# Negated row maxima turned by VectorE's 32x32 block transpose instead of TensorE, and written to the query stack by four transfers per half batch

## What is computed

```
attn = jnp.einsum('blhd,bmhd->bhlm', q, k) / scale
p = jax.nn.softmax(attn, axis=-1)
o = jnp.einsum('bhlm,bmhd->blhd', p, v).reshape(B, L, D)
```

## Time and profile before

| what | value |
|---|---|
| median of the runs | 1639.73 us |
| profiled execution's own time | 1638.78 us |
| span of its trace | 1637.0 us |
| TensorE matmul busy | 1542.3 us, 94% |
| VectorE busy | 1044.1 us, 64% |
| ScalarE busy | 779.4 us, 48% |
| GpSimd busy | 182.1 us, 11% |
| mean granted TensorE clock | 0.989 |

### The profile page before, as it was taken

The page is one execution under the profiler, slowest core; times in us unless marked ns, Lnnn a source line. Parts: engine busy times, 40 slices in busy tenths (PEclk is TensorE's granted clock), DMA queues, the critical chain, the costliest instruction groups (busy, mean ns, idle before and its releaser), DMA issues. The chain is left out here.

```text
span 1637.0 us, 30596 instructions
## 1 busy us (share of the span) xinstructions
PE 1542.3 (94%) x10971; PEld 1287.6 (79%) x11020; DVE 1044.1 (64%) x3343; ACT 779.4 (48%) x1684; POOL 182.1 (11%) x219
## 2 busy tenths in 40 slices
PE   2569999999999999999999999999999999999997
PEld 1458888888888888888888787887877778777785
DVE  7746555555555555555567767776676776767773
ACT  1335444444444444444445555555555555555554
POOL 7400000000000000000000000000001011110102
PEclk9789999999999999999999999999999999999999
DMA  7074222222222222221235445354453444444340
GB/s 264 7 91 66 44 40 46 46 40 44 47 46 47 47 47 41 37 52 31 40 67 66 69 60 70 51 70 66 60 73 57 76 73 66 85 64 83 69 71 21
DMA packets 99584, 100.09 MB, mean 61 GB/s; under 512 B 11478, under 2 KB 96088, under 8 KB 98794
## 3 DMA queue, kind: packets, MB, share of 16 engines
q1 hardware_dynamic: 99434, 98.14, 36.2%
HBM read 16.83 MB, written 4.19 MB: 13 GB/s over the span
## 5 line engine op out<-in xcount | busy, mean ns | idle before, releaser
L922 ACT ACTIVATE work<-bank 128x512 f32<-128x512 f32 x768 | 453.6, 600 | 244.1 <-PE bank L1116 201.2
L528 DVE TENSOR_REDUCE rowmax<-bank 128x2 f32<-128x512 f32 x512 | 342.9, 687 | 167.7 <-PE bank L1099 163.1
L1116 PE MATMUL bank<-qs,ks 98*128 98x256 f32 x1536 | 401.9, 344 | 0.9 <-DVE rowmax L528 0.6
L1099 PE MATMUL bank<-ks,qs 96*128 96x256 f32 x1536 | 349.8, 310 | 12.7 <-DMA ks<-qk_lo 10.3
L1116 PEld LDWEIGHTS bank<-qs,ks 98*128 98x128 f32 x1536 | 270.2, 192 | 33.2 <-issue 12.4
L1099 PEld LDWEIGHTS bank<-ks,qs 96*128 96x128 f32 x1536 | 243.7, 190 | 39.1 <-DMA ks<-qk_lo 14.7
L525 DVE CUSTOM_DVE_ANT_0 c1t<-bank,big_q 128x256 bf16<-128x256 f32 x512 | 190.4, 421 | 0.7 <-issue 0.7
L1128 PE MATMUL bank<-work,vp 128*32 128x256 f32 x3072 | 185.7, 382 | 0.0
L1128 PEld LDWEIGHTS bank<-work,vp 128*32 128x32 f32 x3072 | 89.9, 109 | 66.1 <-issue 6.0
L948 ACT ACTIVATE work<-bank 128x256 f32<-128x256 f32 x128 | 49.3, 385 | 192.3 <-PE bank L1175 192.3
L1175 PE MATMUL bank<-yt,w_gate 128*128 128x256 f32 x512 | 131.8, 379 | 2.1 <-ACT yt L942 2.1
(11 more groups left out here) (208 smaller groups left out, 1891.9 us busy)
## 6 DMA issues: line engine op xcount, KB each, us to landing
qs<-qk_hi SPq DMA_DIRECT2D x192, 128.0 KB, 3.9
ks<-qk_hi SPq DMA_DIRECT2D x192, 128.0 KB, 3.8
qs<-qk_lo SPq DMA_DIRECT2D x96, 128.0 KB, 4.3
ks<-qk_lo SPq DMA_DIRECT2D x96, 128.0 KB, 4.3
xres<-in_x_t SPq DMA_DIRECT2D x4, 1024.0 KB, 9.5
x_in<-in_x SPq DMA_DIRECT2D x16, 256.0 KB, 3.2
out<-xres SPq DMA_DIRECT2D x16, 256.0 KB, 2.1
qs<-nm SPq DMA_DIRECT2D x96, 16.0 KB
```

The source lines that it names most:

```text
L528: a = dve.tensor_reduce(rowmax[:, :, k:k + 1], bank[:, :].rearrange("p (t s) -> p t s", t=TC), AX, ALU.max)
L922: act.activation(probs[:, place[n, b, k], :, :], bank[:, :].rearrange("p (c s) -> p c s", c=TC), ACT.Exp, scale=HD ** -0.5)\
L1099: m = pe.matmul(bank[:, t * S:(t + 1) * S], qs[par][0:SCORE_ROWS, k, t * P:(t + 1) * P], ks[par][0:SCORE_ROWS, k, :], start=True, stop=True)
L1116: m = pe.matmul(bank[:, c * S:(c + 1) * S], ks[par][0:SHIFTED_ROWS, k, c * P:(c + 1) * P], qs[par][0:SHIFTED_ROWS, k, :], start=(n != 3), ...
```

## The change

`nm` and `negs` get the same shape of 128 partitions by 32 columns, with columns ordered (part, head, token tile). After L537 VectorE waits for the low part and for the earlier DMAs out of `nm`, and transposes each 32x32 block of `negs` in its own quadrant of 32 partitions into `nm` (new line L538, STREAM_TRANSPOSE). Row r of quadrant w then holds column r of `negs` for tokens 32w to 32w+31 of a tile. The two TensorE transposes, their bank use in the ring, and the copy L542 are gone. SP issues four DMAs for each half batch, one for each quadrant w; each writes pieces of 32 numbers (128 bytes) to rows 96 and 97 of `qs`, where the one DMA of before wrote runs of 256 numbers. The bytes are the same. `probs` waits for all four. `SLOT` and `LATER` get other numbers for several steps in all three layers.

```diff
+QUADS = P // HW
 SLOT:  (two of the lines, layer 2)
-        "smax": -14.7, "pv": (9.43, 16.76), "neg": (-6.67, 1.15), "max": (-6.24, 2.71), ...
+        "smax": -15.46, "pv": (9.43, 16.53), "neg": (-6.97, 0.53), "max": (-6.04, 2.71), ...
...
-        negs = [sb(f"negs{u}", [P, TC, 2 * HALF], F32R) for u in range(DC)]
-        nm = [sb(f"nm{u}", [2 * HALF, S], F32R) for u in range(DC)]
+        negs = [sb(f"negs{u}", [P, 2, HALF, TC], F32R) for u in range(DC)]
+        nm = [sb(f"nm{u}", [P, 2 * HALF * TC], F32R) for u in range(DC)]
...
-                self.shifted = [shared(f"shifted{u}", 16) for u in range(DC)]
+                self.shifted = [shared(f"shifted{u}", 16 * QUADS) for u in range(DC)]
...
-                if what == "max":
-                    return [(middle, f"max{k}", self.nm, k + 1)]
...
                     if what == "neg":
-                        top = rowmax[:, :, HALF * k:HALF * (k + 1)]
-                        hi, lo = negs[k][:, :, 0:HALF], negs[k][:, :, HALF:2 * HALF]
+                        top = rowmax[:, :, HALF * k:HALF * (k + 1)].rearrange("p t h -> p h t")
+                        hi, lo = negs[k][:, 0, :, :], negs[k][:, 1, :, :]
...
-                    if what == "max":
-
-                        bank = middle.wait_filled(dve, n, b, f"max{k}")
+                        dve.wait_ge(L.negs.sem, L.negs.at(b, 2 * k + 2))
                         dve.wait_ge(L.shifted[k].sem, L.shifted[k].at(b, 0))
-                        dve.tensor_copy(nm[k][:], bank[0:2 * HALF, 0:S]).then_inc(L.nm.sem, 1)
+                        dve.transpose(nm[k][:].bitcast(F32), negs[k][:].rearrange("p a h t -> p (a h t)").bitcast(F32)).then_inc(L.nm.sem, 1)
...
                     if what == "max":
                         sp.wait_ge(L.nm.sem, L.nm.at(b, k + 1))
-                        sp.dma_start(qs[par][SHIFT:SHIFT + 2, HALF * k:HALF * (k + 1), :].bitcast(F32), nm[k][:].bitcast(F32)).then_inc(L.shifted[k].sem, 16)
+                        shift = qs[par][SHIFT:SHIFT + 2, HALF * k:HALF * (k + 1), :].rearrange("p h (t w c) -> p h t w c", t=TC, w=QUADS)
+                        for w in range(QUADS):
+                            rows_w = slice(HW * w, HW * (w + 1))
+                            sp.dma_start(shift[:, :, :, w, :].bitcast(F32), nm[k][rows_w, :].bitcast(F32)).then_inc(L.shifted[k].sem, 16)
...
-                    if what == "max":
-
-                        pe.wait_ge(L.negs.sem, L.negs.at(b, 2 * k + 2))
-                        bank = middle.wait_free(pe, n, b, f"max{k}")
-                        for t in range(TC):
-                            m = pe.transpose(bank[0:2 * HALF, t * P:(t + 1) * P], negs[k][:, t, :].bitcast(F32), ident[:])
-                        m.then_inc(middle.sem, 1)
```

More of the change, by code:

```diff
@@ L38 @@
     1: {
-        "smax": -13.9, "pv": (8.35, 15.57), "neg": (-6.64, 1.59), "max": (-6.11, 3.88), "xT": -26.05, "q": -24.15,
-        "stack": (-25.3, -22.08, -15.9, -16.88), "k": -22.83, "v": -12.48, "tok": 18.52, "load": -46, "rank": -33,
-        "cond": -31.71, "squares": -30.67, "xn": -28.51, "oT": 20.77, "wo": 22.0, "yn": 23.31, "yT": 24.73,
+        "smax": -13.9, "pv": (8.35, 15.57), "neg": (-6.64, 2.63), "max": (-6.11, 3.88), "xT": -26.05, "q": -24.15,
+        "stack": (-25.3, -22.08, -15.9, -16.88), "k": -22.83, "v": -12.48, "tok": 18.52, "load": -46, "rank": -32.97,
+        "cond": -31.71, "squares": -30.67, "xn": -28.51, "oT": 20.77, "wo": 22.51, "yn": 23.31, "yT": 24.73,
         "ffn": (25.73, 1.15), "down": (26.94, 1.15)},
     2: {
[6 rows of a table removed]
-        "squares": 22.77, "resid": 24.18},
[6 rows of a table added]
+        "wo": 22.34, "squares": 23.07, "resid": 24.21},
 }
-LATER = {"vector": {"q": -0.2, "k": 0.5, "ffn": 0.3, "oT": 0.39, "field": -0.34, "pv": -0.22, "coh2": 0.07, "squares": 0.41}, "scalar": {"wo": 1.0, "pv": 0.2, "yn": -0.02, "oT": -0.25, "xn": -0.04, "ffn": -0.24, "xT": -0.5, "field": 0.3, "k": -0.14}, "gpsimd": {"max": -0.28, "oT": -0.2, "q": -0.42, "pv": -0.5}, "sync": {"wo": 0.39}}
+LATER = {"vector": {"q": -0.2, "k": 0.5, "ffn": 0.3, "oT": 0.39, "field": -0.34, "pv": -0.22, "coh2": 0.07, "squares": 0.41}, "scalar": {"wo": 1.0, "pv": 0.2, "yn": -0.02, "oT": -0.25, "xn": -0.04, "ffn": -0.24, "xT": -0.5, "field": 0.44, "k": -0.14, "squares": -0.13, "coh2": -0.04}, "gpsimd": {"max": -0.28, "oT": -0.2, "q": -0.42, "pv": -0.5}, "sync": {"wo": 0.39}}
 ONCE = {"ortho": -33.5, "top": -30.3, "shares": -26.5, "spread": -22.0}
@@ L1101, in step @@
                         m.then_inc(middle.sem, 1)
-                    if what == "max":
-                        pe.wait_ge(L.negs.sem, L.negs.at(b, 2 * k + 2))
-                        bank = middle.wait_free(pe, n, b, f"max{k}")
-                        for t in range(TC):
-                            m = pe.transpose(bank[0:2 * HALF, t * P:(t + 1) * P], negs[k][:, t, :].bitcast(F32), ident[:])
-                        m.then_inc(middle.sem, 1)
                     if what == "probs":
                         if k % HALF == 0:
-                            pe.wait_ge(L.shifted[k // HALF].sem, L.shifted[k // HALF].at(b, 16))
+                            pe.wait_ge(L.shifted[k // HALF].sem, L.shifted[k // HALF].at(b, 16 * QUADS))
                         bank = back.wait_free(pe, n, b, f"p{k}")
```

## The result

The changed kernel took 1627.26 us (median of 5 runs, 1624.28 to 1629.49) against 1639.73 us before (median of 5 runs): ratio 0.9928, 95% interval 0.9914 to 0.9943. It is 12.5 us faster. The forecast was 32 us faster, with a range of 1591 to 1624 us, so the direction was right and the size was wrong. The profiled execution took 1626.92 us, its span 1625.1 us.

What follows compares the result with a forecast made beforehand. TensorE was taken as the bound; 6.7, 11.8 and 16.2 us gained in layers 1 to 3 (34.7), less 3 for VectorE, gave about 32 us off 1639.7, so 1607.5 us, with an 8-in-10 range of 1591 to 1624.

Steps and rivals of the forecast that it cites:

- TensorE is the bound, and its freed slots are the gain: All layers: each pair of transposes leaving TensorE frees 0.21 us where nothing waits; 96 pairs, 20.2 us.
- The stall for the negation goes: Layers 2 and 3: TensorE's wait ahead of the transposes goes, 0.53 and 0.80 us in one half batch per batch.
- the first rival: TensorE's 15.8 us idle for the negation returns as waits for maxima or exponentials; gain only 20.2 us, 1619.5; chance 0.20.
- the give-back: Layer 3: VectorE is next to be late once TensorE no longer waits; 0.2 us a batch, 3 us in all.
- VectorE's part: VectorE swaps the 409 ns copy L542 for a block transpose of 200 ns, relieving it by some 20 us.
- SP's three more issues cost nothing: SP issues 1.95 us more per half batch; cost nothing, bounds -0.3 to +1.95 us a batch of layer 2.
- The one on SP's queue: Key stack pushed back the full 1.95 us, TensorE waiting that much more per layer 2 batch: +31 us, 1648 total; chance 0.07.
- Small pieces: Rival: 128-byte pieces double the nm transfers' landing to 5.8 us, delaying probs; 42 us in layer 2, 1659 total; chance 0.03.

Runs made afterwards that it cites:

- l3_stack_first: Changed kernel, but in layer 3 SP issues the key stack for heads 0 to 7 before the output store and four nm transfers: 1600.87 us, ratio 0.9775.

## Why the prediction was wrong

- *TensorE is the bound, and its freed slots are the gain.* Right in kind. The pair costs 0.21 us in layer 1, as forecast (5.2 us gained over 15 periods, 6.3 forecast). In layers 2 and 3 putting the pair back cost 0.12 and 0.11 us, not 0.21.
- *The stall for the negation goes.* Right: the row is gone. The idle time didn't come back as a wait for maxima on the matmul side, as the first rival had it. With the stack out of the way (l3_stack_first), layer 3 lost 16.4 us against before, where 15 of the 16 forecast periods come to 15.2 us. Layer 2 lost 15.8 us in the changed kernel, with 11.1 forecast for 15 periods. Once layer 3 doesn't wait, the span is 1637.0 - 1598.8 = 38.2 us shorter, where 34.7 less 3 given back to VectorE were forecast; the give-back isn't seen.
- *VectorE's part.* Right: 211 ns against 200 taken, and never over 214, though it stands next to negations of 1.22 us.
- *SP's three more issues cost nothing.* This is the step that failed, and by its second half. For layer 2 I counted from issue to need, found the margin nearly zero, and the new place of the negation covered it, as the rows after show (2.5 us of matmul wait against 2.0). For layers 1 and 3 I wrote that "no wait for the stack stands in the rows, and SP itself spends most of its time waiting, so I cost the issues at nothing there". Layer 1 bore it: its rows after have no wait for the stack. Layer 3 had 1.5 us of slack in the batch shown, took 1.2 us of later issue, 0.8 us of TensorE's own earliness and 0.5 us of later landing, and paid 18.3 us of waits in 13 batches. Its order put right (l3_stack_first) gives 24.8 us back: 18.4 of idle time, some 5 of lower clock by estimate, and a rest. So the term that stood at nothing measured about 25 us. The sum with it is 34.7 - 24.8 = 10 us, and 12.5 were measured.
- *The rivals.* The one on SP's queue was the right mechanism with 0.07 of the chance, priced in layer 2, where it cost little; of layer 3 it said only that lateness there would decide too. "SP waits most of the time" was no argument: its waits stand ahead of `nm` and of the store, and the stack is behind them.
- *Small pieces.* Their landing didn't double. In a batch of layer 2 of the kernel after (SyncE's issues and TensorE's weight load), the fourth issue ends at 999.79 and the `probs` that needs it starts at 1002.88 without a wait, so the fourth transfer lands within 3.1 us of the end of its issue, or 3.8 us of its start, where the one transfer of before landed within 2.9 us. A rise of up to 0.9 us isn't excluded:

```profile
997.14 2.65 SPq L681 DMA_DIRECT2D qs<-nm  x4
999.90 1.24 SPq L666 DMA_DIRECT2D ks<-qk_hi  x2
...
1002.88 0.31 PEld L1108 LDWEIGHTS bank<-qs,ks 98*128 98x128 f32 x2
```

What stays open: why the key transfers of layer 3 land later in the changed kernel, by over 1 us in five batches; why the granted clock fell behind three of five waits over 2 us and not behind the others; and what part of layer 2's surplus of 5 us is owed to the slots and what to the free bank of the ring, which no run separates.

## What to carry to other kernels

When a change adds issues to an in-order DMA queue, take every transfer behind them and measure, from the trace of before, the time from its issue to its first use, less its own landing time (and not that of a like transfer in another layer; the landing can also move with the change, as it did here). A wait of zero in the rows says nothing of how much slack there is; and if the change also makes the consumer earlier, subtract that too. If a transfer has little slack, put it ahead of the new issues: that one line of order was worth about 25 us here (1627.3 to 1600.9 by the medians), twice what the change had brought.

## What the runs showed of the hardware

- An issue of a transfer from `nm` takes SyncE about 0.65 us whether it carries 16 pieces of 1 KB or 32 of 128 bytes (four take 2.65 us); four with 4 KB in pieces of 1 KB took 2.57 us. An issue of 128 KB of the stack takes 0.60 us. The number of issues counts, not the bytes.
- The landing of the 128 KB stack transfers depends on what was issued ahead. The last key transfer for heads 0 to 7, third of its kind in a row, landed in 3.9 us in layer 3 before (median of 13), in 4.3 with the store and four small transfers ahead, and in 3.9 with either moved behind. In l3_stack_first, where it is the sixth of its kind in a row, it landed in 5.4 us. A median over all of them (4.1 before, 5.6 after) mixes these places.
- A wait of about 2 us on TensorE can cost more than itself: behind three of five such waits the lower clock was granted (a mean of 0.57 to 0.66 over windows of 4 to 5 us), and such a batch lasted 28.3 to 28.9 us where one with a wait of 1.1 us lasted 25.8.
- VectorE's block transpose of 128x32 fp32 took 211 to 214 ns in all 96 places, where the two negations ahead of it reached 885 and 1224 ns. No run shows what spares it.
